# Reading the moving operand of a split matmul product backwards, last column first

## The reference, cut to what matters

```
# feed-forward, on n = layernorm(x), prev = n of the token before
xr = mu_r * n + (1 - mu_r) * prev ;  xk = mu_k * n + (1 - mu_k) * prev
x = x + 0.5 * sigmoid(xr @ W_r.T) * (relu(xk @ W_k.T) ** 2 @ W_v.T)
# attention, on n = layernorm(x)
q, k = relu(n @ Wq.T) / 4, relu(n @ Wk.T) / 4 ;  v = n @ Wv.T ;  u = silu(n @ Wu.T)
out = q @ (k.T @ v)                      # per sequence and head
x = x + (srms_norm(out) * u) @ Wo.T
```

## Time and profile before

| | |
|---|---|
| median of 3 runs | 313.84 us (313.24 to 313.97) |
| profiled execution | 313.0 us, of which the span from the first to the last instruction is 311.3 us |
| busy: PE, PEld, DVE, ACT, POOL | 304.1, 278.4, 240.2, 235.5, 213.7 us |
| granted TensorE clock | 1.000 |

### The profile page before, as it was taken

The page is one execution under the profiler, slowest core; times in us unless marked ns, Lnnn a source line. Parts: engine busy times, 40 slices in busy tenths (PEclk is TensorE's granted clock), DMA queues, the critical chain, the costliest instruction groups (busy, mean ns, idle before and its releaser), DMA issues.

```text
span 311.3 us, 5822 instructions
## 1 busy us (share of the span) xinstructions
PE 304.1 (98%) x2044; PEld 278.4 (89%) x2044; DVE 240.2 (77%) x586; ACT 235.5 (76%) x461; POOL 213.7 (69%) x236
## 2 busy tenths in 40 slices
PE   6999999999999999999999999999999999999995
PEld 5688889989988988988989998989999999999984
DVE  3989884575756845995894699586979797999695
ACT  2896959779589579679359448669797979699981
POOL 4487977779678687669169314825797979758833
PEclk9999999999999999999999999999999999999999
DMA  7950000000000000000000000000001010101023
GB/s 220 380 210 2 1 3 0 0 2 0 3 0 3 0 0 2 0 2 0 2 1 1 2 0 0 2 1 3 0 3 67 2 67 25 45 2 67 33 105 135
DMA packets 10752, 10.85 MB, mean 35 GB/s; under 512 B 482, under 2 KB 10724, under 8 KB 10724
## 3 DMA queue, kind: packets, MB, share of 16 engines
q1 hardware_dynamic: 10432, 10.23, 9.6%
q10 hardware_dynamic: 292, 0.26, 0.3%
HBM read 6.29 MB, written 4.19 MB: 34 GB/s over the span
## 4 chain that ended last, share of the span: by engine, by line
PE 94%; DVE 4%; issue 1%; POOL 0%; ACT 0%; DVEq 0%; POOLq 0%; ACTq 0%
PE psK L1276 9%; PE psK L1278 9%; PE psK L1277 9%; PE psRV L1276 8%; PE psRV L1277 8%; PE psRV L1278 8%; PE psX L1276 8%; PE psX L1277 8%; PE psX L1278 8%; PE psA L1293 4%; PE psX L1493 2%; PE psK L1480 2%; PE psA L1480 2%; PE psX L1407 2%; PE psRV L1518 1%; PE psRV L1383 1%
## 5 line engine op out<-in xcount | busy, mean ns | idle before, releaser
L945 DVE SCALAR_TENSOR_TENSOR mix<-psA,mu,mix 128x512 f32<-128x512 f32 x60 | 41.5, 743 | 11.7 <-ACT mix L632 11.7
L615 ACT ACTIVATE xn<-xs,shiftA,rstdA 128x256 f32<-128x256 f32 x53 | 27.7, 607 | 15.9 <-POOL shiftA L408 15.9
L424 POOL TENSOR_TENSOR mix_k_lo<-mix,mix_k_hi 128x512 fp32r<-128x512 f32 x26 | 33.2, 1296 | 8.7 <-ACT mix_k_hi L665 8.7
L632 ACT ACTIVATE mix<-psA,one_mu 128x511 f32<-128x511 f32 x60 | 36.9, 698 | 0.6 <-PE psA L1293 0.6
L1276 PE MATMUL psRV<-ffn_hi,mix_r_hi 128*128 128x256 f32 x120 | 34.7, 289 | 0.0
L1278 PE MATMUL psRV<-ffn_hi,mix_r_lo 128*128 128x256 f32 x120 | 33.9, 283 | 0.0
L1277 PE MATMUL psRV<-ffn_lo,mix_r_hi 128*128 128x256 f32 x120 | 33.9, 283 | 0.0
L1276 PE MATMUL psRV<-ffn_hi,act_hi 128*128 128x256 f32 x96 | 27.7, 289 | 0.0
L1278 PE MATMUL psRV<-ffn_hi,act_lo 128*128 128x256 f32 x96 | 27.1, 283 | 0.0
L1277 PE MATMUL psRV<-ffn_lo,act_hi 128*128 128x256 f32 x96 | 27.1, 283 | 0.0
L476 POOL TENSOR_TENSOR k_lo<-k_tok,k_hi 128x512 fp32r<-128x512 f32 x14 | 18.1, 1292 | 11.7 <-ACT k_hi L719 11.7
(11 more groups left out here) (204 smaller groups left out, 1085.0 us busy)
## 6 DMA issues: line engine op xcount, KB each, us to landing
xs<-x_dram SPq DMA_DIRECT2D x7, 512.0 KB, 7.9
out_dram<-xs SPq DMA_DIRECT2D x7, 512.0 KB, 2.9
out_dram<-xs SPq DMA_DIRECT2D x4, 128.0 KB, 1.8
xs<-x_dram ACTq DMA_DIRECT2D x2, 128.0 KB, 2.8
xs<-x_dram SPq DMA_DIRECT2D x2, 128.0 KB, 2.6
silu_u<-w_ffn_k_dram SPq DMA_DIRECT2D x1, 256.0 KB, 4.1
silu_u<-w_ffn_r_dram SPq DMA_DIRECT2D x1, 256.0 KB, 6.6
q_store<-w_k_dram SPq DMA_DIRECT2D x1, 256.0 KB, 6.8
```

What stands on the lines that cost most here:

```text
L424: nc.gpsimd.tensor_tensor(mix_k_lo[:, h, :], mix[:, 0, h, :], mix_k_hi[:, h, :].bitcast(F32), ALU.subtract).then_inc(s_lo_k, 1)
L615: nc.scalar.activation(xn[:, t, :], tile_row(xs, b, t), ACT.Identity, bias=shiftA[:, t:t + 1], scale=rstdA[:, t:t + 1]).then_inc(s_xn, 1)
L632: nc.scalar.activation(mix[:, rk, h, 1:BLOCK], psA[:, h, 0:BLOCK - 1], ACT.Copy, scale=one_mu[:, rk, h:h + 1]).then_inc(s_prev, 1)
L945: nc.vector.scalar_tensor_tensor(out=m, in0=psA[:, h, :], scalar=mu[:, rk, h:h + 1], in1=m, op0=ALU.mult, op1=ALU.add).then_inc(s_mix, 1)
```

## The change

`product` turns three of its five access patterns round: the accumulator `dst` and both halves of the moving operand are given from the last column to the first, so each steps by one element backwards. The stationary operands stay as they are. Where the moving operand has two dimensions of columns (`k_and_u`), both are turned, so that the 512 columns are one run backwards there too. Column c of the moving operand still makes column c of the result; only the order in time is turned round. The number of instructions, their order on each engine, their shapes, the semaphores and the places of all tensors are the same; in the program built from the change all rows of TensorE stand in the same order, with lines below the helper moved down by four (the three matmuls are L1280 to L1282).

```
         @block.tensor
         def _(pe):
+            def from_the_end(ap):
+                return ap[:, ::-1] if len(ap.shape) == 2 else ap[:, ::-1, ::-1]
+
             def product(dst, a_hi, a_lo, b_hi, b_lo, start, stop):
+                dst, b_hi, b_lo = (from_the_end(ap) for ap in (dst, b_hi, b_lo))
                 nc.tensor.matmul(dst, a_hi, b_hi, start=start, stop=False)
                 nc.tensor.matmul(dst, a_hi, b_lo, start=False, stop=False)
                 return nc.tensor.matmul(dst, a_lo, b_hi, start=False, stop=stop)
```

## The result

The changed kernel takes 314.63 us (median, 314.45 to 314.82), the kernel before 313.84 us (313.18 to 314.38): a ratio of 1.003, with a 95% interval from 1.0016 to 1.0044. It is slower by 0.8 us, a quarter of a per cent: small, but outside the noise. The forecast of 313.8 us said no change.

A forecast was written before the change was run, and what follows sets the result against it. TensorE was taken to bound the kernel through its split matmuls' pace; 311.3 + 0 + 0 + 0 us of span, 313.0 us with 1.7 us around it, set to the median of 313.8 us. Range 304 to 330 us.

The forecast's parts named there:

- no change: Likeliest case for the whole kernel: time stays at 313.8 us, own range 312.9 to 314.8, chance 0.50.
- What bounds the kernel: TensorE, busy 304.1 of 311.3 us with hardly a wait; the split matmuls' pace arrives at the end nearly in full.
- The first term, the direction of the reads: Backwards reads of the moving operand in 1548 split matmuls: taken as 0, bounded above by 198 us.
- Half the rate: Rival: backwards reads or writes in split matmuls take two clocks per column, adding 198 us, 512 us; chance 0.18.
- the two bounds: For the moving operand's backwards reads: from below nothing, from above the plain float32 matmuls' two clocks per column, 198 us.
- the price per column: Split matmuls: the prediction called itself wrong if a run's direction costs anything per column; it took 0.
- The second term, the writes: Backwards writes into PSUM by the same 1548 matmuls: taken as 0, same bounds as the reads, not payable twice.
- The third term, where an access begins: Split accesses beginning at an operand's last element, not a multiple of 512 bytes: taken as 0, above 13.9 or 27.9 us.
- prices of 9 and 18 ns: Upper bounds per split matmul for another beginning, from group mean durations: 13.9 or 27.9 us over all 1548.
- The price per matmul: Rival: every split matmul pays some ns before its first column; 1548 x 9 ns = 13.9 us, 327.7 us; chance 0.21.
- The gain: Rival: turning one stream round parts moving reads from weight loads; up to 17.5 us, about half arriving, 305 us; chance 0.11.
- the 13 ns: Time each split matmul takes beside one clock per column, at 256 and 512 columns alike; no row explained it.

The follow-up runs named there:

- e1: Kernel before with moving operand and accumulator turned round only in the 512-column products: 315.18 us, against 313.84 us before.
- e9: Kernel before, all forwards, with only the tensors that are moving in 256-column products (ffn, wo, k) 508 bytes past a multiple of 512: 312.27 us.
- e12: Kernel before with only 512-column products changed: moving operand and accumulator take groups of four words last to first, forwards inside each: 315.60 us.
- e14: Kernel before with only 512-column products changed: first 256 columns backwards, then second 256 backwards, in moving operand and accumulator: 315.64 us.
- e2: Kernel before with moving operand and accumulator turned round only in the 256-column products: 312.62 us, against 313.84 us before.
- e4: Kernel before with only the accumulator written backwards, the moving operand read forwards: 313.79 us, ratio 0.9995 to 1.0012.
- e11: Kernel before, all forwards, with only the tensors that are moving in 256-column products (ffn, wo, k) 16 bytes past a multiple of 512: 312.64 us.
- e16: Kernel before, all forwards, with 512-column moving operands at multiples of 512 bytes and all other split operands 508 bytes on: 311.89 us, 0.9946 of before.
- e7: Kernel before, all forwards, with the stationary operands of the 256-column products 256 bytes past a multiple of 512: 313.79 us.
- e10: Kernel before, all forwards, with only the tensors that are moving in 256-column products (ffn, wo, k) 4 bytes past a multiple of 512: 315.85 us.
- e6: Changed kernel, backwards, with all split operands 4 bytes on, so backwards reads begin at a multiple of 512 bytes: 316.66 us, against 313.84 us before.
- e13: Kernel before with only 512-column products changed: groups of four words ascending, words inside each backwards, in moving operand and accumulator: 313.81 us.

## Why the prediction was wrong

**What bounds the kernel** was right: the split matmuls' pace arrives at the end for the most part, in both directions (in the traces all of the 0.8 us of the changed kernel, 1.85 of 2.1 in e1, 1.4 of 1.9 in e9), and TensorE has no wait that it hadn't before.

**The first term, the direction of the reads, is the step that failed for the sign.** Half the rate is refuted, at 118 and 233 ns, so the choice between the two bounds was right. But "I take nothing, which is the nearer end as far as pattern goes: a run of neighbouring words stays one" put at nothing what made the kernel slower: in the 512-column products, descending from group to group costs 6.7 ns per matmul once the pace has settled (e1, e12, e14), 2.2 us over all of them. It isn't the price per column that the forecast named as its sign of being wrong: with 256 columns, from byte 508 and with the weights in their places, backwards takes 118.3 ns (e2) and forwards 117.5 (e9).

**The second term, the writes**, was right: e4 shows nothing.

**The third term, where an access begins, failed as well, the other way.** It was put at nothing too, and it gave 1.4 us back at the 256-column products of the changed kernel (1.2 us in the medians of e2). "I take nothing here too, since psX and psK halves that begin at different offsets run at one pace": that looked at where accumulators begin, which is the side that doesn't matter, while in every row of before every moving operand of a split product begins at a multiple of 512 bytes, and so do those halves. Its prices of 9 and 18 ns came from durations, which overlap; the settled distances of the changed kernel moved by 6.7 ns at most. The rows couldn't show what another beginning costs, and the term should have kept its width. Moved to byte 508 by itself, in a forwards read, the beginning makes a 256-column matmul 2.5 ns faster (e9).

**The rivals.** The price per matmul was nearest the truth, but it was to be "the same few ns more at 256 and at 512 columns", and the two lengths went opposite ways. The gain was half of the truth: turned round alone, the 256-column products did get faster (e2), and the guess that all operands at multiples of 512 bytes are part of the 13 ns is borne out by e9, e11 and e16, at 3 of the 13 ns at most. That the weights' place is the partner in this e7 doesn't bear out for the 256-column products; for `ffn_k` e10 shows that it counts.

So what came out near no change was the sum of +2.2 and -1.4 us, neither of which the forecast had; that the time came within 0.8 us of it, inside the 312.9 to 314.8 us given for no change, is luck. **What stays open** is why. The pace of a split matmul depends on where its moving read begins, on whether a long one descends, and on where its weights lie (e10), by up to 7 ns each; e6, descending and with the weights 4 bytes on, adds 10. That the read and the load meet in some way would fit this and isn't shown: the runs don't show what inside the chip makes it so.

## What to carry to other kernels

A layout tuned to one alignment isn't tuned for all lengths: try where the moving operand begins for each length by itself, as 3 ns per matmul were worth 1.9 us here (e16 against before), and an offset of 4 bytes cost 2 us. Shift the weights by themselves too, since 4 bytes took `ffn_k` from 227 to 232 ns (e10). When a change turns round or moves all products alike, look at the pace of each shape apart, since a time that hardly moves can be a gain and a loss. And a term for which all rows stand at one setting is unknown, not nothing.

## What wasn't expected of the hardware

- Plain float32 matmuls pay 2 ns beside their columns, split ones 10 to 23 ns: 116.7 to 122.5 ns for 106.7 ns of columns, and 226.7 to 236.7 for 213.3, by the address and direction of the moving read and the address of the weights.
- A moving read of 256 columns from byte 4 of a 512-byte block takes 122.5 ns or a little more, from byte 0 120.0, from byte 16 118.8, from byte 508 117.5.
- Writing PSUM with a step of minus one is free (e4), and so is the order of the words within 16 bytes of a moving read (e13); descending from one 16 bytes to the next costs 6.7 ns in 512 columns (e12).
